# One read of each expert's weights: GpSimd rounds the high part by a copy and subtracts in place of a second, rounding transfer

## The chip, the cores and the metric

The kernel runs on one core of one Trainium2 chip. The metric is the device time of one execution in microseconds, as the median of several runs; lower is better. The engines are named as in the profile: PE is TensorE (PEld its weight loads), DVE is VectorE, ACT is ScalarE, POOL is GpSimd and SP is SyncE, which here only issues transfers.

## The reference, cut to what matters

A gated cross-attention block on x of 4 x 512 x 512 is followed by a mixture of experts. Every token goes to 4 of 16 experts; each expert is a gated feed-forward layer of width 352, and a shared one of width 704 runs for all tokens.

```python
x = x + tanh(g_xattn) * xattn(layernorm(x), ctx, ctx, wq, wk, wv, wo)
x = x + tanh(g_ffn) * moe(layernorm(x), Wg, W1, W2, W3, W1s, W2s, W3s)

# moe: 2048 tokens, 16 experts, top 4, D = 512, FF = 352
shared = silu(x @ W1s.T) * (x @ W3s.T) @ W2s.T
probs = softmax(x @ Wg.T);  topk_w, sel = top_k(probs, 4)
combine = zeros((T, E)).at[arange(T)[:, None], sel].add(topk_w)
h = silu(einsum('td,efd->etf', x, W1)) * einsum('td,efd->etf', x, W3)
routed = einsum('etf,edf->td', h * combine.T[:, :, None], W2)
return shared + routed
```

## The kernel before

The kernel keeps float32 accuracy with three products for each one: every operand is split into a high part, rounded to the type that PE multiplies (`fp32r`), and a low part, raw minus high; `tripled` (L80) issues high x high, low x high and high x low. For weights the high part comes from a transfer on POOL's queue that rounds on its way (`expert_hi`), the raw values from a second transfer of the same bytes (`expert_raw`), and POOL subtracts: `expert_lo = expert_raw - expert_hi`. `expert_raw` and `expert_lo` lie at one address, so the subtraction is in place.

There are four phases, each a block that all engines leave together. In attention (to about 458 us of the span) nothing here is touched. In the second phase, called routing (458 to 577 us; tiles and names with `b_`), PE runs the shared feed-forward for half of the tokens in two rounds n of six column groups j (the matmuls of one group write `b_ps_u`), then four outputs (`b_ps_y`). DVE multiplies gate and value of a group (L928, `b_h`), which also frees the PSUM buffer that PE's group after the next needs, and takes the low part of the group before (L917, `b_h_lo`, both inputs in SBUF). Between the groups DVE does the routing: at n = 0, j = 0 it ranks the experts of the last 512 tokens (L98 to L107, mostly with two inputs in SBUF) and makes `mask` (L1206), on which PE's counting matmuls ahead of group 3 wait (L1247); at j = 1 it makes the rest of the shared down weights' low part (L979); and so on, until lists of one-hot rows give every tile its tokens (`slot_tokens`). POOL in that time subtracts for the shared down weights (L979, 128x2560) and for the first expert (L964: 128x3840 and then 96x512), and issues loads.

In the third phase, experts (577 to 1061 us, `c_`), the tokens are sorted by expert into tiles of 128: 72 tiles here, four or five for each expert. For a tile t, PE transposes the gathered rows `xg` (L1447), multiplies with `expert_hi` and `expert_lo` (`c_ps_u`), does the down product of tile t - 2 and the transposes of tile t - 1. POOL runs one `step` for each tile, in order: wait until PE has transposed tile t, gather tile t + 4 into the buffer that this frees (L1338, an indirect transfer), and, where tile t is the first of its expert e, make the low part of expert e + 1 and issue the loads of expert e + 2. Three buffers of weights go round. All of POOL's transfers, gathers and weight loads, go through one queue. PE waits with `w_ready` for an expert's low part, and with `gathered` for a tile's rows.

The last phase (from 1077 us, `d_`) runs the shared feed-forward for the other half and adds up the experts' outputs.

Of the kernel before, what the change touches and what calls it, by code (L numbers as in the profile page):

```python
# [13 lines left out]
P = 128  # L14
B, S, D = 4, 512, 512
T = B * S
NT = T // P
IT = S // P
# [4 lines left out]
FT = FF - 2 * P  # L23
# [715 lines left out]
W13 = 2 * DC * FF  # L739
W2 = 2 * D  # L740
WE = W13 + W2 + D
# [207 lines left out]
def part(w, rows, base, start, n):  # L949

    return w[0:rows, base + start:base + start + n] if isinstance(base, int) else w[0:rows, bass.ds(base + start, n)]


def load_expert(eng, w, base, io, e, sem):

    eng.dma_start(part(w, P, base, 0, W13 + W2), io["we"][e]).then_inc(sem, 16)
    eng.dma_start(part(w, FT, base, W13 + W2, D), io["we_rest"][e]).then_inc(sem, 16)


def split_expert(eng, later, base, sem):  # L960

    for rows, start, n in ((P, 0, W13 + W2), (FT, W13 + W2, D)):
        hi, lo, raw = (part(w, rows, base, start, n) for w in (later.w_hi, later.w_lo, later.w_raw))
        last = eng.tensor_tensor(lo, raw, hi, ALU.subtract)  # L964
    last.then_inc(sem, 1)
# [16 lines left out]
def routing_phase(nc, io, mem, keep, later):  # L982


    with ExitStack() as c:
# [51 lines left out]
        def _(sp):  # L1037
# [17 lines left out]
            sp.wait_ge(keep["gathered"][0], 16)  # L1055
            load_expert(sp, later.w_raw, WE, io, 1, keep["second_raw_in"])


        @block.gpsimd
        def _(pool):  # L1060
# [15 lines left out]
            load_expert(pool, later.w_hi, 0, io, 0, hi_in["first"])  # L1076
# [3 lines left out]
            pool.wait_ge(hi_in["first"], 32)  # L1080
            pool.wait_ge(raw_in["first"], 32)
            split_expert(pool, later, 0, first_ready)

            pool.wait_ge(sh.t_free, 2 * IT)
            pool.wait_ge(hot_ready, 1)
            load_expert(pool, later.w_hi, WE, io, 1, keep["w_in"])
# [4 lines left out]
                ap=keep["index"][:, 0:1], axis=0)).then_inc(keep["gathered"][0], 16)  # L1091
        @block.scalar
        def _(act):
            sh.scalar(act)
# [174 lines left out]
def expert_phase(nc, io, mem, keep, later):  # L1269

    with ExitStack() as c:
# [62 lines left out]
        def _(pool):  # L1334
# [6 lines left out]
            def load(base, e):  # L1341

                load_expert(pool, later.w_hi, base, io, e, w_in)
                load_expert(pool, later.w_raw, base, io, e, w_in)

            def step(t, v):
# [9 lines left out]
                with pool.If(flag > 0):  # L1356
# [3 lines left out]
                    pool.wait_ge(w_in, e * 64 + 32)  # L1360
                    split_expert(pool, later, base, w_ready)
# [16 lines left out]
            pool.wait_ge(keep["second_raw_in"], 32)  # L1378
# [242 lines left out]
def program(nc, io, out):  # L1621
    mem = {k: nc.dram_tensor(k + "_dram", shape, F32, kind="Internal").ap() for k, shape in (
        ("x2", [T, D]), ("xn2", [T, D]), ("base", [T, D]), ("y", [(TILES_MAX + REST) * P, D]))}
    keep = persistent(nc)
    later = Later(nc, keep["end"])
    with ExitStack() as c:
# [6 lines left out]
        keep["w_in"], keep["second_raw_in"] = sem("w_in"), sem("second_raw_in")  # L1633
# [47 lines left out]
```

## Time and profile before

| what | us |
|---|---|
| median of 3 runs | 1194.11 |
| lowest and highest run | 1193.88, 1196.51 |
| span of the profiled execution | 1198.8 |
| PE busy | 1117.1 (93%) |
| DVE busy | 508.4 (42%) |
| POOL busy | 467.2 (39%) |
| ACT busy | 280.2 (23%) |
| read from HBM, written to it | 161.51 MB, 37.75 MB |

The profiled execution has no time of its own beside its span, 1198.8 us from its first instruction to its last; that is 4.7 us over the median and 2.3 us over the highest of the three runs. Times inside the profile are positions in that span. PE is busy for nearly all of it, so that what shortens the kernel is a stretch in which PE stands still or runs at a lower clock; the other engines matter by what they keep PE waiting for.

### The profile page before, as it was taken

The numbers are of one execution on the slowest core, as the hardware profiler recorded it, in microseconds if no ns is written. First come the engines' busy times: TensorE is split into PE (matmuls) and PEld (weight loads), VectorE is DVE, ScalarE is ACT, GpSimd is POOL, SyncE is SP. The second block draws the span as 40 slices with busy tenths as digits, with TensorE's granted clock in tenths as the row PEclk, the third lists the DMA queues.
The fourth block names the chain that finished last, engine by engine and source line by source line (L and its number), as shares of the span: only waits on it lengthen the run. The fifth ranks groups of instructions, "written<-read, shape, count | busy, mean of one in ns | idle before, by whom it ended". The sixth has DMA issues, their size and how long they took to land. (4 is left out here: it accounts for less than half of the span.)

```text
span 1198.8 us, 18625 instructions
## 1 busy us (share of the span) xinstructions
PE 1117.1 (93%) x5666; PEld 948.6 (79%) x5667; DVE 508.4 (42%) x994; ACT 280.2 (23%) x575; POOL 467.2 (39%) x464
## 2 busy tenths in 40 slices
PE   4999998999899968799889999999999999989998
PEld 3877876878687845677779999999999999977675
DVE  2243446336443454999212222222222222226847
ACT  1221121113112201211123333333333333321110
POOL 4610101200210223300564565565656665608752
PEclk9998998999899977999889999999999999999898
DMA  9411221221120517140856666665666656526775
GB/s 358 169 71 70 73 98 41 105 105 70 37 103 35 219 71 265 38 138 32 292 219 230 223 223 223 223 222 196 247 227 215 231 214 232 201 80 227 234 249 158
DMA packets 54208, 199.70 MB, mean 167 GB/s; under 512 B 7008, under 2 KB 7008, under 8 KB 45984
## 3 DMA queue, kind: packets, MB, share of 16 engines
q0 software_dynamic: 21184, 122.44, 29.3%
q1 hardware_dynamic: 22624, 57.98, 13.5%
q10 hardware_dynamic: 10368, 18.88, 4.2%
q8 instruction: 18, 0.29, 0.1%
q14 instruction: 14, 0.11, 0.0%
HBM read 161.51 MB, written 37.75 MB: 166 GB/s over the span
## 5 line engine op out<-in xcount | busy, mean ns | idle before, releaser
L86 PE MATMUL c_ps_u<-expert_hi,xT_hi 128*128 x576 | 192.6, 334 | 1.7 <-DVE xT_lo L1421 1.6
L86 PE MATMUL c_ps_u<-expert_hi,xT_lo 128*128 x576 | 185.9, 323 | 0.0
L86 PE MATMUL c_ps_u<-expert_lo,xT_hi 128*128 x576 | 185.6, 322 | 0.0
L964 POOL TENSOR_TENSOR expert_lo<-expert_raw,expert_hi (+2 forms) x32 | 156.0, 4896 | 19.8 <-issue 13.3
L86 PEld LDWEIGHTS c_ps_u<-expert_hi,xT_hi 128*128 128x128 f32 x576 | 108.8, 189 | 2.4 <-issue 2.3
L1435 DVE TENSOR_TENSOR hf<-c_ps_u,gate 128x352 f32<-128x352 f32 x72 | 37.7, 524 | 169.8 <-ACT gate L1410 169.8
L86 PEld LDWEIGHTS c_ps_u<-expert_lo,xT_hi 128*128 128x128 f32 x576 | 109.3, 190 | 0.0
L86 PEld LDWEIGHTS c_ps_u<-expert_hi,xT_lo 128*128 128x128 f32 x576 | 108.8, 189 | 0.0
L1425 DVE TENSOR_TENSOR hT_lo<-c_ps_h,hT_hi 128x256 fp32r<-128x256 f32 x72 | 30.5, 424 | 182.0 <-ACT hT_hi L1400 182.0
L73 POOL TENSOR_TENSOR idle<-idle 128x1 f32<-128x1 f32 x91 | 17.4, 191 | 225.9 <-PE c_ps_x L1447 141.9
L86 PE MATMUL c_ps_y<-expert_hi,hT_hi 128*128 (+1 forms) x216 | 92.5, 428 | 2.3 <-DVE hT_lo L1426 2.3
L86 PE MATMUL c_ps_y<-expert_lo,hT_hi 128*128 (+1 forms) x216 | 86.2, 399 | 0.0
L86 PE MATMUL c_ps_y<-expert_hi,hT_lo 128*128 (+1 forms) x216 | 86.2, 399 | 0.0
L1338 POOL DMA_INDIRECT xg<-xn_dram,column x72 | 71.4, 992 | 25.1 <-issue 19.8
L1572 POOL DMA_INDIRECT parts<-y_dram,token_slots x64 | 68.2, 1065 | 27.2 <-issue 19.2
L1410 ACT ACTIVATE gate<-c_ps_u 128x352 f32<-128x352 f32 x72 | 33.5, 465 | 180.9 <-PE c_ps_u L86 180.9
L1393 ACT ACTIVATE y<-c_ps_y 128x512 f32<-128x512 f32 x72 | 43.1, 599 | 114.6 <-PE c_ps_y L86 114.6
L407 DVE TENSOR_TENSOR q_lo<-ps_products,q_hi 128x512 fp32r<-128x512 f32 x32 | 22.1, 690 | 101.7 <-ACT q_hi L339 101.7
L339 ACT ACTIVATE q_hi<-ps_products 128x512 fp32r<-128x512 f32 x32 | 19.1, 598 | 154.4 <-PE ps_products L86 154.4
L1421 DVE TENSOR_TENSOR xT_lo<-c_ps_x,xT_hi 128x512 fp32r<-128x512 f32 x72 | 49.8, 691 | 12.6 <-ACT xT_hi L1387 9.3
L1599 DVE SCALAR_TENSOR_TENSOR total<-parts,combine_weights,total 128x512 f32<-128x512 f32 x64 | 48.0, 751 | 14.3 <-DMA total<-x_dram 8.1
L569 PE MATMUL ps_transposed<-ident,x_t 128*128 128x128 f32 x80 | 16.5, 357 | 40.0 <-DVE x_t L425 39.3
(268 smaller groups left out, 2480.1 us busy)
## 6 DMA issues: line engine op xcount, KB each, us to landing
expert_hi<-we POOLq DMA_DIRECT2D x16, 1920.0 KB, 7.9
expert_raw<-we POOLq DMA_DIRECT2D x14, 1920.0 KB, 13.0
y_dram<-y ACTq DMA_DIRECT2D x72, 256.0 KB, 2.1
ctxT_hi<-ctxT POOLq DMA_DIRECT2D x4, 1024.0 KB, 7.4
ctxT_raw<-ctxT SPq DMA_DIRECT2D x4, 1024.0 KB, 5.9
ctx_raw<-ctx SPq DMA_DIRECT2D x4, 1024.0 KB, 4.8
r_t<-x SPq DMA_DIRECT2D x4, 1024.0 KB, 5.4
ctx_hi<-ctx POOLq DMA_DIRECT2D x4, 1024.0 KB, 6.8
```

Of the source, the lines that this page charges most:

```text
L86: last = pe.matmul(out, a[i], b[j], start=(n == 0), stop=(n == 3 * len(pairs) - 1))
L339: act.activation(out, ps_m[:, (m.n - 1) % 2, :], ACT.Copy).then_inc(m_hi, 1)
L407: dve.tensor_tensor(lo, ps_m[:, (m.n - 1) % 2, :], hi, ALU.subtract).then_inc(m_free, 1)
L964: last = eng.tensor_tensor(lo, raw, hi, ALU.subtract)
L1338: pool.indirect_dma_start(xg[v][:], None, mem["xn2"], bass.IndirectOffsetOnAxis(ap=at, axis=0)).then_inc(gathered[v], 16)
L1393: act.activation(y[v][:], ps_y[:, v % 2, :], ACT.Copy).then_inc(y_taken, 1)
L1410: act.activation(gate[u][:], ps_u[:, u, 0, 0:FF], ACT.Silu).then_inc(gate_ready, 1)
L1421: dve.tensor_tensor(x[u][1][:], ps_x[:], x[u][0][:], ALU.subtract).then_inc(x_split, 1)
L1425: dve.tensor_tensor(h[u][1][:, 0:2, :], ps_h[:, 0:2, :], h[u][0][:, 0:2, :], ALU.subtract)
L1435: dve.tensor_tensor(hf[u][:], ps_u[:, u, 1, 0:FF], gate[u][:], ALU.mult).then_inc(h_ready, 1)
L1572: pool.indirect_dma_start(parts[v][:, q, :], None, y_d, bass.IndirectOffsetOnAxis(ap=keep["slots"][:, order[c], q:q + 1], axis=0)).then_in ...
L1599: ins = dve.scalar_tensor_tensor(out=total[k][:], in0=parts[c % 4][:, q, :], scalar=keep["weights"][:, order[c], q:q + 1], in1=total[k][:] ...
```

## The change

The rounding transfer of each expert's weights is gone: `expert_hi` is made by POOL, with `tensor_copy` from `expert_raw`, in the same two pieces as the subtraction. A wait on a new semaphore (`hi_made`) and a small instruction (`hold`) stand between the copies and the subtractions. The raw load of the second expert leaves SP, where it waited for the first gather, and is issued by POOL right behind that gather. POOL no longer waits for it ahead of the first tile, but in the first step.

```diff
-def split_expert(eng, later, base, sem):
-
+def split_expert(nc, keep, eng, later, base, expert, sem):
+
+    made = keep["hi_made"]
+    for rows, start, n in ((P, 0, W13 + W2), (FT, W13 + W2, D)):
+        hi, raw = (part(w, rows, base, start, n) for w in (later.w_hi, later.w_raw))
+        last = eng.tensor_copy(hi, raw)
+    last.then_inc(made, 1)
+    eng.wait_ge(made, expert + 1)
+    hold(nc, eng, keep, 6)
     for rows, start, n in ((P, 0, W13 + W2), (FT, W13 + W2, D)):
         hi, lo, raw = (part(w, rows, base, start, n) for w in (later.w_hi, later.w_lo, later.w_raw))
         last = eng.tensor_tensor(lo, raw, hi, ALU.subtract)
...
-            sp.wait_ge(keep["gathered"][0], 16)
-            load_expert(sp, later.w_raw, WE, io, 1, keep["second_raw_in"])
...
-            load_expert(pool, later.w_hi, 0, io, 0, hi_in["first"])
             pool.wait_ge(hi_in["down"], 32)
             pool.wait_ge(raw_in["down"], 32)
             split_down(pool, later.d_hi, later.d_lo, later.d_raw, True, down_ready)
-            pool.wait_ge(hi_in["first"], 32)
             pool.wait_ge(raw_in["first"], 32)
-            split_expert(pool, later, 0, first_ready)
-
-            pool.wait_ge(sh.t_free, 2 * IT)
-            pool.wait_ge(hot_ready, 1)
-            load_expert(pool, later.w_hi, WE, io, 1, keep["w_in"])
+            split_expert(nc, keep, pool, later, 0, 0, first_ready)
 
             pool.wait_ge(index_ready, 1)
             pool.wait_ge(sh.u_ready, 2 * SC)
             pool.indirect_dma_start(later.xg[0][:], None, mem["xn2"], bass.IndirectOffsetOnAxis(
                 ap=keep["index"][:, 0:1], axis=0)).then_inc(keep["gathered"][0], 16)
+            load_expert(pool, later.w_raw, WE, io, 1, keep["w_in"])
...
-                load_expert(pool, later.w_hi, base, io, e, w_in)
                 load_expert(pool, later.w_raw, base, io, e, w_in)
...
-                    pool.wait_ge(w_in, e * 64 + 32)
-                    split_expert(pool, later, base, w_ready)
+                    pool.wait_ge(w_in, e * 32 + 32)
+                    split_expert(nc, keep, pool, later, base, e + 1, w_ready)
...
-            pool.wait_ge(keep["second_raw_in"], 32)
             last = tiles(pool, step)
```

On POOL, at the place of the routing phase where the first expert is split, this stood before (`xg_69` is the first tile's gather, `slot_tokens` the list that it reads):

```order
L956 DMA expert_hi<-we 128x3840
L957 DMA expert_hi<-we_rest 96x512
L979 TENSOR_TENSOR shared_down_lo<-shared_down_raw,shared_down_hi 128x2560
L964 TENSOR_TENSOR expert_lo<-expert_raw,expert_hi 128x3840
L964 TENSOR_TENSOR expert_lo<-expert_raw,expert_hi 96x512
L956 DMA expert_hi<-we 128x3840
L957 DMA expert_hi<-we_rest 96x512
L1090 DMA xg_69<-xn_dram,slot_tokens 128x512
```

and this stands there now:

```order
L986 TENSOR_TENSOR shared_down_lo<-shared_down_raw,shared_down_hi 128x2560
L965 CAST expert_hi<-expert_raw 128x3840
L965 CAST expert_hi<-expert_raw 96x512
L73 TENSOR_TENSOR idle<-idle 128x1
L971 TENSOR_TENSOR expert_lo<-expert_raw,expert_hi 128x3840
L971 TENSOR_TENSOR expert_lo<-expert_raw,expert_hi 96x512
L1087 DMA xg_69<-xn_dram,slot_tokens 128x512
L956 DMA expert_raw<-we 128x3840
L957 DMA expert_raw<-we_rest 96x512
```

Two rounding loads are gone from here, two casts and a small instruction have come in ahead of the subtractions, and the second expert's raw load, from SP's queue, stands behind the gather.

On POOL, in the step of a tile that is the first of its expert, from the subtraction to the gather of the next step (the rows of registers and branches between are left out), this stood before:

```order
L964 TENSOR_TENSOR expert_lo<-expert_raw,expert_hi 128x3840
L964 ISA
L964 TENSOR_TENSOR expert_lo<-expert_raw,expert_hi 96x512
...
L956 DMA expert_hi<-we 128x3840
L957 ISA
L957 DMA expert_hi<-we_rest 96x512
L956 REGISTER_ALU
L956 DMA expert_raw<-we 128x3840
L957 REGISTER_ALU
L957 DMA expert_raw<-we_rest 96x512
...
L1338 DMA xg_70<-xn_dram,column_3353 128x512
```

and this stands there now:

```order
L965 COPY expert_hi<-expert_raw 128x3840
L965 ISA
L965 COPY expert_hi<-expert_raw 96x512
L967 REGISTER_ALU
L73 TENSOR_TENSOR idle<-idle 128x1
L971 TENSOR_TENSOR expert_lo<-expert_raw,expert_hi 128x3840
L971 TENSOR_TENSOR expert_lo<-expert_raw,expert_hi 96x512
...
L956 DMA expert_raw<-we 128x3840
L957 ISA
L957 DMA expert_raw<-we_rest 96x512
...
L1337 DMA xg_70<-xn_dram,column_3349 128x512
```

The next tile's gather now has two loads ahead of it in the queue instead of four, and two copies more ahead of it on the engine.

## Rows read from the trace of the kernel before

**Rows 1.** Stretch, its us, busy PE PEld DVE ACT POOL, clock, DMA share, GB/s.

```profile
630.00:1060.00 430.00, 430.00 (x2573) 400.36 (x2572) 117.35 (x256) 139.60 (x320) 249.71 (x294) 1.00 0.62 219
```

**Rows 2.** PE's waits: what ended them, us in total, times, longest.

```profile
PE c_ps_x L1447 <- DMA xg<-xn_dram,column: 4.5, 1, 4.5
```

**Rows 3.** PE's timeline, transposes of tiles 3 to 6 of the experts.

```profile
597.66 0.60 PE L1447 MATMUL c_ps_x<-ident,xg 128*128 128x128 f32 x4
604.36 0.60 PE L1447 MATMUL c_ps_x<-ident,xg 128*128 128x128 f32 x4
615.78 1.11 PE L1447 MATMUL c_ps_x<-ident,xg 128*128 128x128 f32 x4 [4.50 <-DMA xg<-xn_dram,column]
624.75 0.60 PE L1447 MATMUL c_ps_x<-ident,xg 128*128 128x128 f32 x4
```

**Rows 4.** The same view as rows 1, behind PE's wait in the experts.

```profile
615.78:622.00 6.22, 6.22 (x23) 5.11 (x24) 0.69 (x1) 1.26 (x3) 4.22 (x4) 0.63 0.24 77
```

**Rows 5.** POOL's timeline at the start of the experts.

```profile
577.28 0.98 POOL L1338 DMA_INDIRECT xg<-xn_dram,slot_tokens  x1 [0.17 <-issue]
...
585.88 0.19 POOL L1349 COPY column<-slot_tokens 128x1 int32<-128x1 int32 x1 [5.12 <-DMA expert_raw<-we_rest]
...
589.75 9.76 POOL L964 TENSOR_TENSOR expert_lo<-expert_raw,expert_hi  x2 [1.88 <-issue]
...
601.24 0.54 POOL L957 DMA_DIRECT2D expert_raw<-we_rest  x1
...
602.81 1.01 POOL L1338 DMA_INDIRECT xg<-xn_dram,column  x1 [0.50 <-issue]
```

**Rows 6.** Transfers issued from 599 to 603 us: KB, us from issue to landing.

```profile
expert_hi<-we_rest POOLq DMA_DIRECT2D x1, 192.0 KB, 9.0
expert_raw<-we_rest POOLq DMA_DIRECT2D x1, 192.0 KB, 13.8
```

**Rows 7.** Landing of the gather issued at 602.81 us.

```profile
DMA to landing us min/median/max: 12.9/12.9/12.9
```

**Rows 8.** SP's queue at the end of routing: start, us.

```profile
575.25 0.43 SPq L956 DMA_DIRECT2D expert_raw<-we  x1
```

**Rows 9.** POOL's casts in the profile before: us in total, mean ns.

```profile
L1074 POOL CAST lane<-lane_i 128x128 f32<-128x128 int32 x1 | 0.3, 298 | 0.0
L1075 POOL CAST token<-token_i 128x16 f32<-128x16 int32 x1 | 0.2, 202 | 0.0
```

**Rows 10.** POOL's timeline in routing, 470 to 495 us.

```profile
470.46 5.71 POOL L979 TENSOR_TENSOR shared_down_lo<-shared_down_raw,shared_down_hi 128x2560 fp32r<-128x2560 f32 x1 [8.05 <-DMA shared_down_hi<-d_rest]
482.68 10.07 POOL L964 TENSOR_TENSOR expert_lo<-expert_raw,expert_hi 128x3840 fp32r<-128x3840 f32 x2 [6.52 <-DMA expert_raw<-we_rest]
```

**Rows 11.** DVE's timeline in the same stretch.

```profile
472.11 5.14 DVE L98 TENSOR_TENSOR b_rank_level<-probs 128x1024 f16<-128x1024 f32 x1
...
478.54 1.23 DVE L102 TENSOR_TENSOR b_rank_level<-probs 128x1024 f16<-128x1024 f32 x1
...
481.78 0.23 DVE L107 TENSOR_TENSOR ranks<-b_rank_larger,b_rank_equal 128x64 f32<-128x64 f32 x1
...
482.25 0.68 DVE L928 TENSOR_TENSOR b_h<-b_ps_u,b_silu 128x512 f32<-128x512 f32 x1
482.85 8.78 DVE L917 TENSOR_TENSOR b_h_lo<-b_h,b_h_hi 128x512 fp32r<-128x512 f32 x1
...
493.33 0.69 DVE L928 TENSOR_TENSOR b_h<-b_ps_u,b_silu 128x512 f32<-128x512 f32 x1
```

**Rows 12.** PE's timeline there: the wait of group 4.

```profile
494.08 0.80 PE L86 MATMUL b_ps_u<-b_xT_hi,shared_up_hi 128*128 128x512 f32 x1 [5.32 <-DVE b_h L928]
```

**Rows 13.** The same view as rows 1, routing's start and behind PE's wait.

```profile
458.00:482.00 24.00, 21.65 (x88) 17.15 (x86) 13.09 (x11) 5.64 (x9) 9.94 (x14) 0.82 1.03 366
...
494.08:497.50 3.42, 3.42 (x8) 2.75 (x9) 3.25 (x8) 0.61 (x1) 0.00 (x0) 0.50 0.00 0
```

**Rows 14.** First expert's last raw piece, issued from SP at 460.8 us.

```profile
expert_raw<-we_rest SPq DMA_DIRECT2D x1, 192.0 KB, 21.8
```

More of the change, by code:

```diff
@@ L1632, in program @@
         keep["y_out"], keep["base_out"] = [sem(f"y_out{v}") for v in range(QUAD)], [sem(f"base_out{u}") for u in range(2)]
-        keep["w_in"], keep["second_raw_in"] = sem("w_in"), sem("second_raw_in")
+        keep["w_in"], keep["hi_made"] = sem("w_in"), sem("hi_made")
         keep["last_down_in"], keep["last_xs_in"] = sem("last_down_in"), [sem(f"last_xs{i}_in") for i in range(IT)]
```

## The prediction

> **What bounds the kernel now.** I read first the busy times by stage. From 630 to 1060 us PE is busy for 430.00 of 430 us at the full granted clock [rows 1]. Nothing that POOL or the transfers do can shorten that part; it can only break it. So I looked for the places where PE stands still and where POOL's work or the weight loads have a hand in it. The list of PE's waits and its timeline give two.
>
> The first is in the experts. PE waits 4.5 us for a gather of rows, once, and nowhere else there [rows 2]. The timeline shows what that costs in all: the transposes of tile 3 and tile 4 stand 604.36 - 597.66 = 6.70 us apart, which is the length of a tile, while from tile 4 to tile 6 it takes 624.75 - 604.36 = 20.39 us instead of 13.40 [rows 3]. The tile costs 7.0 us too much: 4.5 of waiting, and about 2.5 more at a lower clock (0.63 of full on average behind the wait [rows 4]). The gather is late because of POOL. POOL waited 5.12 us for the second expert's raw load, subtracted for 9.76 us, issued four loads and only then, at 602.81, this gather [rows 5]. It landed 12.9 us later [rows 7], at 615.7, which is 0.7 us behind the last piece of those loads (601.24 + 13.8 = 615.0 [rows 5, 6]).
>
> The second is in routing. PE waits 5.32 us for DVE's `b_h` of group 2 [rows 12] and then runs 3.4 us at 0.50 of the clock [rows 13], so at 1.2 instead of 2.4 GHz, which loses 1.7 us. DVE is late because its instructions with two inputs in SBUF stood still while POOL subtracted: L98 took 5.14 us beside POOL's 5.71 us subtraction and ended 1.1 us behind it, though its twin L102 takes 1.23; L917 took 8.78 us beside POOL's next one [rows 10, 11]. DVE came through its ranking undisturbed only because POOL's second subtraction began at 482.68, right behind `b_h` of group 1 at 482.25.
>
> **The change in the experts.** SP no longer issues two transfers at the end of routing; they began at 575.25, each of some 0.43 us [rows 8], and with the gap between them the end of the phase comes 0.9 us earlier. POOL then does not stand for 5.12 us, so its first `column` copy, at 585.88 before, comes at 585.88 - 5.12 - 0.9 = 579.9, and its first work on weights 3.87 us later (589.75 - 585.88 [rows 5]), at 583.7. The data are there by then: the raw load is issued before the phase ends, by 575 at the latest, and an unburdened load's last piece lands 9.0 us after issue [rows 6].
>
> The price of the copies is what the trace does not show at this size. The lower bound is from POOL's casts: (298 - 202) ns for (128 - 16) elements is 0.86 ns per element [rows 9], which makes 3.5 us for 128x3840 and 0.6 us for 96x512, 4.1 us together. The upper bound is that a copy costs as much as the subtraction of the same size, 9.76 us for both [rows 5]; that instruction reads twice as much, so I take 4.1. The wait on `hi_made` and `hold` add 0.4 us, an estimate from the 0.50 us that POOL idles between such a small instruction and the gather at 602.81 [rows 5].
>
> So the copies end at 587.8, the subtractions run from 588.2 to 598.0. Before, the last raw piece was issued 1.73 us and the gather 3.30 us after the subtractions' end; with two issues of about 0.55 us fewer this is 0.6 and 2.2 us. The raw load's last piece lands at 598.6 + 9.0 = 607.6, the gather, again 0.7 us behind it, at 608.3. PE wants it at 604.36 + 6.70 - 0.9 = 610.2. The margin is 1.9 us: the stall goes, -7.0 us, and the earlier end of routing gives -0.9.
>
> For the other experts the chain from one load to the next is copies 4.1, 0.4, subtractions 9.76, issue 0.6, landing 9.0: 23.9 us, against 4 x 6.70 = 26.8 us for the shortest experts. It stays hidden under PE, and so do the gathers, which have half as many bytes ahead of them. Were that cover gone (the upper bound makes it 29.6), each such expert would bring POOL 2.8 us later.
>
> **The change in routing.** One load of 1920 + 192 KB fewer competes. The stretch from 458 to 482 moved 366 GB/s [rows 13], so 2.16 MB are worth 5.9 us, and the first expert's last raw piece, at 460.8 + 21.8 = 482.6 before [rows 14], lands at about 476.7. POOL's down subtraction ends at 476.17 [rows 10]. Hence POOL starts on the expert at about 477.3, behind DVE's waiting L98, and not at 482.68. That is worse for DVE, whose whole ranking now runs beside it. One after the other, by the rows and with the port changing hands at each instruction: copy to 480.8; L102 (ready at 478.54) to 482.0; second copy to 482.6; L103 to 483.3; POOL's large subtraction, 8.3 us (482.68 to 482.85 + 8.78 - 0.68), from 483.4 to 491.7; only then L107, ready long ago, then `mask`, and `b_h` of group 1 at 493.0 instead of 482.9 [rows 11]. PE's group 3 needs both and starts 10.1 us late. Group 4's wait of 5.32 us is no longer there, since `b_h` of group 2 follows within 3 us. Net +4.8, and 0.4 for a somewhat longer stretch at the lower clock behind a wait twice as long: +5.2 us.
>
> Whether a copy, with its one input, holds DVE off too, no row shows; only subtractions do. The Trainium skill (GPSIMD Engine Reference, section 8, Key points) says that GpSimd shares its SBUF interfaces with VectorE, in contention with VectorE's instructions that have two inputs in SBUF, and makes no exception for GpSimd's one-input ones. By it the copies block and the sum stays as above; it is a rule against this change. With the subtractions alone blocking, the term is +2.5 (first rival).
>
> **Sum.** -7.0 - 0.9 + 5.2 = -2.7 us. The profiled span of 1198.8 becomes 1196.1. The span lies 4.7 us over the median of the runs, and the same difference put on 1194.1 gives 1191.4. Its own range, for copies of 4 to 6 us and a raw load that lands within 2 us of my time, is 1188.5 to 1194.5. A difference under 0.2% (2.4 us) can't be told from none.
>
> **Rivals.**
> - Copies do not hold DVE. They run at 476.7 to 480.8, the large subtraction from 481.2 to 489.5 still catches L107 (ready at 481.78), `b_h` of group 1 ends at 490.7, 7.8 us late, less 5.3: +2.5. Time 1188.7. For it: no row of a one-input POOL instruction that stops DVE. Against: all long POOL instructions in the trace did.
> - The raw load lands late, after 482.3. Then DVE's ranking passes, `b_h` of group 2 slips in between the copies and the large subtraction, and PE waits about 3.3 us at group 5 in place of 5.3 at group 4: -2 and -1 for the clock, with the experts' -7.9 that is -10.9 in all, 1183.2. Against it is the sum of bytes.
> - Slower: the copies are dear. Each us over 4.1 costs one in routing, and each beyond the margin of 1.9 another in the experts. The gain is used up at copies of 6.4 us; over 0.2% slower begins at 7.6. At the upper bound routing costs +10.9 and the stall is 3.8 + 2.5 of the old 7.0: 1194.1 + 10.9 - 0.7 - 0.9 = 1203.4, more if four-tile experts in a row fall behind.
> - The gather stays late although the copies are cheap, because a raw load with stores of zeros and gathers beside it lands later than 9.0 + 1.9 us. Then up to the whole 7.0 stays: 1194 to 1198.4.
>
> **Chances.** Forecast 0.45, copies that don't hold DVE 0.19, late raw load 0.07, dear copies 0.17, late gather 0.12. Below 1191.7 lie a little over half of the forecast's case (0.25) and the first two rivals: 0.51 faster. Within 0.2% lie the rest of it and some of the last two: 0.31. Slower 0.18. The range 1186 to 1199 leaves out the late load and the upper end of dear copies.
>
> **What would show it.** In the changed kernel's timeline: the large copy 3.5 us long; no wait of PE on `xg` near 611; POOL's expert work in routing starting at 477 and not 483; L102 stretched to about 3.5 us; L107 ending near 492; one PE wait of about 11 us ahead of the counting matmul and none at group 4; 430 us of unbroken PE afterwards. The prediction is wrong if the copy is 6 us or more, if the first raw load lands after 482, or if POOL's subtraction leaves L107 alone.

## The result, and the profile after

The change made the kernel slower: a median of 1199.77 us (15 runs) against 1196.09 us of the kernel before, run beside it (15 runs; the three runs that stand in the table above had 1194.11). The ratio is 1.0033, with a 95% interval of 1.002 to 1.0046, so 3.9 us. The profiled span went from 1198.8 to 1200.3 us; that pair alone is a poor measure, since single executions of one kernel differ by some us with the granted clock.

The page of the kernel after: busy time, share, instructions, and the bytes.

```profile
PE 1114.9 (93%) x5666; PEld 946.8 (79%) x5667; DVE 509.8 (42%) x994; ACT 279.9 (23%) x575; POOL 516.0 (43%) x482
HBM read 126.91 MB, written 37.75 MB: 137 GB/s over the span
L965 POOL CAST expert_hi<-expert_raw (+2 forms) x32 | 64.2, 2034 | 17.3 <-issue 15.4
```

34.6 MB fewer are read, and POOL is busy for 48.8 us more, less than the 64.2 us of the copies, since it issues 15 pairs of loads fewer, of some 1.15 us each. PE's waits, from 452 to 1090 us (what ended them, us in total, times, longest):

```profile
PE b_ps_y L1246 <- DVE mask L1205: 10.5, 1, 10.5
PE c_ps_x L1444 <- PEq L992: 6.7, 1, 6.7
PE c_ps_x L1444 <- DMA xg<-xn_dram,column: 0.6, 1, 0.6
```

The third line answers to [rows 2]: the 4.5 us for the gather at tile 5 are gone; the 0.6 us are another tile's, near the end. The first was 0.8 us before and stands in place of group 4's 5.32 us [rows 12]. The second was 2.6 us before and is the one that my prediction had not asked about: `PEq` is PE's own sequencer, which stands at the end of the routing block until all engines have left it.

I cut the time of PE into stages by marks that both kernels have: the first `b_ps_u` matmul behind the first transposes, the last `b_ps_y` matmul of routing, the first transposes of the experts, those of tile 1 and of the last tile (tiles are counted from 0). "Gap" is from the last routing matmul to the first transposes of the experts.

| us | before | after | difference |
|---|---|---|---|
| routing | 109.94 | 115.02 | +5.1 |
| gap | 3.01 | 7.11 | +4.1 |
| tile 0 | 8.23 | 8.70 | +0.5 |
| tile 1 to last tile | 474.96 | 469.79 | -5.2 |
| the four together | 596.14 | 600.62 | +4.5 |

What lies ahead of these stages is untouched by the change. In the two profiles it was 1.6 us shorter in after, and behind the experts 1.4 us shorter; both vary as much between executions of other kernels below without following any edit.

POOL and then DVE in the kernel after, in routing; the rows answer to [rows 10, 11]. Start and duration.

```profile
467.76 5.71 POOL L986 TENSOR_TENSOR shared_down_lo<-shared_down_raw,shared_down_hi 128x2560 fp32r<-128x2560 f32 x1 [7.96 <-DMA shared_down_hi<-d_rest]
475.38 4.94 POOL L965 CAST expert_hi<-expert_raw 128x3840 fp32r<-128x3840 f32 x2 [1.92 <-DMA expert_raw<-we_rest]
480.40 0.52 POOL L73 TENSOR_TENSOR idle<-idle 128x1 f32<-128x1 f32 x1
480.88 9.47 POOL L971 TENSOR_TENSOR expert_lo<-expert_raw,expert_hi 128x3840 fp32r<-128x3840 f32 x2
```

```profile
475.83 4.02 DVE L102 TENSOR_TENSOR b_rank_level<-probs 128x1024 f16<-128x1024 f32 x1
479.89 0.98 DVE L103 TENSOR_TENSOR b_rank_level<-b_rank_level,b_lower_index 128x1024 f16<-128x1024 f16 x1
480.90 1.22 DVE L106 TENSOR_REDUCE b_rank_equal<-b_rank_level 128x64 f32<-128x1024 f16 x1
482.16 7.07 DVE L107 TENSOR_TENSOR ranks<-b_rank_larger,b_rank_equal 128x64 f32<-128x64 f32 x1
489.26 1.25 DVE L1205 TENSOR_SCALAR mask<-ranks 128x256 f16<-128x256 f32 x1
```

L102, 1.23 us before, takes 4.02 beside a copy with one input (it starts 0.45 us behind the copy, whose large piece lasts 3.39 us); L107, 0.23 us of work, waits out the large subtraction. The end of the block, POOL first, then the landings of what it issued there (KB, us from issue to landing), then PE:

```profile
573.72 1.07 POOL L1087 DMA_INDIRECT xg<-xn_dram,slot_tokens  x1 [83.36 <-DVE slot_tokens L1228]
574.80 0.62 POOL L956 DMA_DIRECT2D expert_raw<-we  x1
575.39 0.57 POOL L957 DMA_DIRECT2D expert_raw<-we_rest  x1
584.18 0.52 POOL L1334 MEMSET zeros<- 128x512 f32 x1 [8.22 <-POOLq L992]
```

```profile
expert_raw<-we POOLq DMA_DIRECT2D x1, 1920.0 KB, 7.9
expert_raw<-we_rest POOLq DMA_DIRECT2D x1, 192.0 KB, 8.3
```

```profile
577.11 0.39 PE L86 MATMUL b_ps_y<-shared_down_hi,b_h_lo 64*128 64x512 f32 x1
584.22 1.09 PE L1444 MATMUL c_ps_x<-ident,xg 128*128 128x128 f32 x4 [6.73 <-PEq L992]
...
612.42 0.60 PE L1444 MATMUL c_ps_x<-ident,xg 128*128 128x128 f32 x4
619.35 0.60 PE L1444 MATMUL c_ps_x<-ident,xg 128*128 128x128 f32 x4
```

The load's last piece lands at 575.39 + 8.3 = 583.7, and POOL and PE start again at 584.2. The same place in the kernel before, SP's issue, its landing, and POOL:

```profile
575.72 0.45 SPq L957 DMA_DIRECT2D expert_raw<-we_rest  x1
expert_raw<-we_rest SPq DMA_DIRECT2D x1, 192.0 KB, 10.1
576.58 0.53 POOL L1335 MEMSET zeros<- 128x512 f32 x1 [5.26 <-POOLq L985]
```

Before, SP issued that piece at 575.72, it landed 10.1 us later, at 585.8, and all engines had started again at 576.6, without waiting for it. So my first reading was: the end of the block waits for the landing of transfers that POOL has issued, and not for those of SP. The last two lines of PE above answer to [rows 3]: tile 4 and tile 5 are 6.93 us apart.

### The profile page after: what moved, and what is told of

The parts are those of the page before. It is cut to its first block and busy times, and to the rows that moved or that the text cites. A ratio compares the mean times of both kernels' runs of the same rounds, so it can differ in the third digit from the quotient of the medians.

```text
span 1200.3 us, 18597 instructions
## 1 busy us (share of the span) xinstructions
PE 1114.9 (93%) x5666; PEld 946.8 (79%) x5667; DVE 509.8 (42%) x994; ACT 279.9 (23%) x575; POOL 516.0 (43%) x482
## 3 DMA queue, kind: packets, MB, share of 16 engines
q1 hardware_dynamic: 22368, 55.81, 12.9%
## 5 line engine op out<-in xcount | busy, mean ns | idle before, releaser
L73 POOL TENSOR_TENSOR idle<-idle 128x1 f32<-128x1 f32 x107 | 21.0, 196 | 173.6 <-PE c_ps_x L1444 88.4
L965 POOL CAST expert_hi<-expert_raw (+2 forms) x32 | 64.2, 2034 | 17.3 <-issue 15.4
L1596 DVE SCALAR_TENSOR_TENSOR total<-parts,combine_weights,total 128x512 f32<-128x512 f32 x64 | 53.8, 840 | 15.0 <-DMA total<-x_dram 8.7
L292 POOL TENSOR_TENSOR ln_rstd<-ln_var,minus_half 128x4 f32<-128x4 f32 x8 | 8.3, 1034 | 109.6 <-DVE ln_var L420 109.6
```

What stands on the lines that cost most here:

```text
L965: last = eng.tensor_copy(hi, raw)
L1596: ins = dve.scalar_tensor_tensor(out=total[k][:], in0=parts[c % 4][:, q, :], scalar=keep["weights"][:, order[c], q:q + 1], in1=total[k][:] ...
```

## The experiments

All stand beside the kernel before, in three groups of four, each on its own chip. The difference in us is the ratio put on 1196; "four stages" is the sum of the stages above, less that of before, from each kernel's one profile.

| kernel | median | ratio [95%] | us | routing | gap | tile 0 | tiles 1 to last | four stages |
|---|---|---|---|---|---|---|---|---|
| before | 1196.0 to 1196.6 | | | 109.94 | 3.01 | 8.23 | 474.96 | |
| after | 1199.77 | 1.0033 [1.002, 1.0046] | +3.9 | 115.02 | 7.11 | 8.70 | 469.79 | +4.5 |
| e1_sp_load | 1199.94 | 1.0032 [1.0016, 1.0048] | +3.8 | 115.12 | 6.05 | 9.14 | 469.22 | +3.4 |
| e2_before_pool_load | 1195.48 | 1.0001 [0.9986, 1.0016] | +0.1 | 109.31 | 8.36 | 9.14 | 469.46 | +0.1 |
| e3_pieces | 1195.94 | 1.0002 [0.9984, 1.002] | +0.2 | 109.68 | 7.46 | 9.40 | 469.83 | +0.2 |
| e4_after_mask | 1199.05 | 1.0023 [1.0007, 1.0038] | +2.8 | 112.44 | 7.45 | 8.12 | 470.90 | +2.8 |
| e7_sp_as_before | 1197.12 | 1.0008 [0.9992, 1.0025] | +1.0 | 114.93 | 3.01 | 8.74 | 469.68 | +0.2 |
| e8_pool_next_phase | 1202.16 | 1.0052 [1.0032, 1.0072] | +6.2 | 115.04 | 2.04 | 11.38 | 473.20 | +5.5 |
| e9_pieces_sp | 1188.53 | 0.995 [0.9934, 0.9966] | -6.0 | 109.58 | 3.01 | 8.38 | 470.18 | -5.0 |
| e10_only_experts | 1188.94 | 0.9941 [0.9921, 0.9962] | -7.1 | 109.47 | 3.02 | 8.46 | 469.17 | -6.0 |
| e11_copies_pieces | 1188.24 | 0.9931 [0.9911, 0.995] | -8.3 | 110.02 | 3.01 | 8.40 | 470.52 | -4.2 |
| e12_subs_pieces | 1190.12 | 0.9941 [0.992, 0.9962] | -7.1 | 108.56 | 3.00 | 8.60 | 471.44 | -4.5 |
| e13_behind_gathers | 1198.43 | 1.001 [0.9992, 1.0028] | +1.2 | 109.48 | 2.04 | 8.60 | 478.51 | +2.5 |
| e14_before_sub_pieces | 1190.18 | 0.9939 [0.9918, 0.9961] | -7.3 | 108.99 | 3.00 | 8.51 | 469.71 | -5.9 |

The stages of single profiles explain the measured differences to 1.4 us but for e11 and e12, which measured 4.1 and 2.5 us faster than their stages say; their intervals are +-2.3 and +-2.5 us wide. Differences of 1 to 2 us between the kernels from e9 to e14 aren't resolved.

### The second raw load from SP, early (e1_sp_load)

```diff
+                if k == 2 * IT - 1:
+                    sp.wait_ge(index_ready, 1)
+                    load_expert(sp, later.w_raw, WE, io, 1, keep["second_raw_in"])
                 sp.wait_ge(sh.y_free, k + 1)
...
                 ap=keep["index"][:, 0:1], axis=0)).then_inc(keep["gathered"][0], 16)
-            load_expert(pool, later.w_raw, WE, io, 1, keep["w_in"])
```

> The changed kernel, with the second expert's raw load issued by SP as soon as the slot list is ready, ahead of its last store, instead of by POOL behind the first gather. Theory (the end of the routing phase waits until the transfers that POOL issued have landed): the gap on PE between the last matmul of routing and the first transposes of the experts falls from 7.1 us to 2 to 3 us, the wait of 10.5 us ahead of the counting matmul stays, and the kernel comes out 4 to 6 us faster than the changed one, so 0 to 2 us under the kernel before. Rival (the gap comes from something else at that place, such as the load's traffic or a late last store): the gap stays near 7 us and the time near +3.9 us.

The gap was 6.05 us and the time that of the changed kernel, as the rival had it. SP's last piece, then POOL, and the landings:

```profile
575.83 0.47 SPq L957 DMA_DIRECT2D expert_raw<-we_rest  x1
```

```profile
575.71 1.07 POOL L1090 DMA_INDIRECT xg<-xn_dram,slot_tokens  x1 [83.43 <-DVE slot_tokens L1230]
585.11 0.53 POOL L1336 MEMSET zeros<- 128x512 f32 x1 [8.33 <-POOLq L992]
```

```profile
expert_raw<-we_rest SPq DMA_DIRECT2D x1, 192.0 KB, 10.5
xg<-xn_dram,slot_tokens POOLq DMA_INDIRECT x1, 9.0
```

POOL now has one transfer outstanding, the first gather. With SP's load just ahead of it, it takes 9.0 us to land and not 3.4; it lands at 584.7, SP's load at 586.3, and the engines start at 585.1, behind the first and ahead of the second. So the load was moved off POOL's queue and the gap stayed, as a gather's late landing. This run doesn't tell the queues apart by its time, only by this order of landings.

### The load alone, put into the kernel before (e2_before_pool_load)

```diff
-            sp.wait_ge(keep["gathered"][0], 16)
-            load_expert(sp, later.w_raw, WE, io, 1, keep["second_raw_in"])
...
                 ap=keep["index"][:, 0:1], axis=0)).then_inc(keep["gathered"][0], 16)
+            load_expert(pool, later.w_raw, WE, io, 1, keep["second_raw_in"])
```

> The kernel before, with only this: the second expert's raw load is issued by POOL behind the first gather, and not by SP. Theory (phase end waits for POOL's transfers to land): PE's gap between routing and experts grows from 3.0 us to about 7 us. Since the load has then landed when the experts start, POOL no longer stands 5.1 us for it, the gather of tile 5 comes about 5 us earlier against PE, and the stall of 7.0 us at tile 5 should shrink to under 1 us; in all -2 to -3 us against the kernel before. Rival (the gap has another cause): the gap stays at 3 us and the time falls by 7 us.

POOL issues the last piece and starts again in the next block:

```profile
569.96 0.59 POOL L957 DMA_DIRECT2D expert_raw<-we_rest  x1
580.02 0.53 POOL L1332 MEMSET zeros<- 128x512 f32 x1 [9.47 <-POOLq L985]
```

The piece landed after 9.4 us, at 579.4, 0.7 us ahead of that start. The gap became 8.36 us, 5.3 us more than before, with no copy in the kernel. The edit also takes 5.5 us of the stall at tile 5 away (tiles 469.46), but all engines now spend about as much in the gap. Both cancel, and the ratio is 1.0001; I had 2 to 3 us less than before.

### First expert's work in pieces (e3_pieces)

```diff
+    pieces = [(P, at, 480) for at in range(0, W13 + W2, 480)] + [(FT, W13 + W2, D)]
-    for rows, start, n in ((P, 0, W13 + W2), (FT, W13 + W2, D)):
+    for rows, start, n in pieces:
         ...
         last = eng.tensor_copy(hi, raw)
...
-    for rows, start, n in ((P, 0, W13 + W2), (FT, W13 + W2, D)):
+    for rows, start, n in pieces:
         ...
         last = eng.tensor_tensor(lo, raw, hi, ALU.subtract)
```

> The changed kernel, with the first expert's copies and subtractions cut into pieces of 480 columns (8 of each in place of one), nothing else. Theory (a POOL instruction holds off a DVE instruction with two inputs in SBUF until it ends, and the two take turns): no such DVE instruction waits more than about 1.3 us, PE's wait of 10.5 us ahead of the counting matmul falls under 2 us and the wait at group 4 of the kernel before does not come back; 10 to 12 us faster than the changed kernel, 6 to 8 us under the kernel before. Rival (DVE is held while POOL has work queued, whatever its pieces, or is slowed in proportion): the wait of PE stays at 8 us or more and the time within 2 us of the changed kernel's.

The wait for the mask falls from 10.5 to 0.4 us. Routing is 5.3 us shorter, not 10: a wait of 3.8 us for `b_h_lo`, later in the phase, comes in. It stands in e9_pieces_sp too, whose rows (PE, then DVE) are:

```profile
499.41 0.50 PE L86 MATMUL b_ps_y<-shared_down_hi,b_h_hi 128*128 128x512 f32 x1 [3.23 <-DVE b_h_lo L917]
```

```profile
487.73 0.53 DVE L1125 COPY r_s<-r_totals 128x256 f32<-128x256 f32 x1
488.30 1.07 DVE L1127 COPY r_s<-r_s 128x16 f32<-128x16 f32 x1
489.29 0.40 DVE L1128 TENSOR_TENSOR r_s<-r_s 128x240 f32<-128x240 f32 x1
489.71 1.08 DVE L1127 COPY r_s<-r_s 128x32 f32<-128x32 f32 x1
...
498.68 0.68 DVE L917 TENSOR_TENSOR b_h_lo<-b_h,b_h_hi 128x512 fp32r<-128x512 f32 x1
```

Behind the mask DVE has some 10 us of small steps for the slots, from 487.7 to 498.1, before it comes to `b_h` and `b_h_lo`. It is busy all that time, but three of the steps (two are shown), copies of 0.2 us in the kernel after, take 1.1 us and a fourth, of 0.35 us, takes 1.5 beside the pieces of the subtraction, 3.8 us too much in all. The hold is spread over these steps and not gone: from `b_h` of group 4 to the end of the next `b_h_lo` DVE takes 13.6 us, against 9.5 in after, and PE waits 3.2 us and then 0.6 more.

### The copies held back until the mask is made (e4_after_mask)

```diff
+            pool.wait_ge(mask_ready, 1)
             split_expert(nc, keep, pool, later, 0, 0, first_ready)
```

> The changed kernel, with POOL waiting for DVE's mask before it starts the first expert's copies. Theory (it was the start of POOL's work, 5.8 us earlier than before, that caught DVE's ranking): the wait ahead of the counting matmul falls from 10.5 us to about 1; DVE's low parts are then held by the copies and by the large subtraction, and PE waits some 3 us at group 4 or 5; 6 to 9 us faster than the changed kernel, 2 to 5 us under the kernel before. Rival (the copies' added 4 us of POOL work are the cause, wherever they lie): PE's waits in routing stay at 9 us or more in sum.

The wait for the mask is gone; waits of 3.1 us for `b_h` and 2.2 for `b_h_lo` are there, since the large instructions now hold DVE at those. Routing 112.44 us: half of the 5.1 us is back, and the time is 1.1 us under the changed kernel's, not 6 to 9. When the large instructions run decides which of DVE's is late, and none of these places is free.

### The second raw load from SP, as before (e7_sp_as_before)

```diff
+            sp.wait_ge(keep["gathered"][0], 16)
+            load_expert(sp, later.w_raw, WE, io, 1, keep["second_raw_in"])
...
                 ap=keep["index"][:, 0:1], axis=0)).then_inc(keep["gathered"][0], 16)
-            load_expert(pool, later.w_raw, WE, io, 1, keep["w_in"])
```

> The changed kernel, but the second expert's raw values are loaded by SyncE, at the place of the kernel before: behind the last store, once the first gather has landed. Theory (the end of the routing phase waits for the landing of what GpSimd has issued, and not for what SyncE has issued): the gap from the last routing matmul to the first expert matmul falls from 7.1 to 3.0 us, and the kernel takes 4 us less than the changed one, about 1195.7 us, a ratio of 1.000 to the kernel before. Rival (the end waits for the load's landing whoever issues it, or something else of the change lengthens the gap): it stays at 6 to 8 us and the time at about 1199.8. In both the stall at tile 5 stays away (experts 469 to 471 us from the second tile to the last).

The gap is 3.01 us again, to the hundredth, with all else as in the changed kernel, and the tiles stay at 469.68. SP, then POOL:

```profile
576.35 0.45 SPq L957 DMA_DIRECT2D expert_raw<-we_rest  x1
```

```profile
577.21 0.53 POOL L1336 MEMSET zeros<- 128x512 f32 x1 [5.27 <-POOLq L992]
...
586.24 3.94 POOL L965 CAST expert_hi<-expert_raw  x2 [2.86 <-DMA expert_raw<-we_rest]
```

The block ends 0.4 us behind SP's last issue, and 9 us before the load is used. The time, +1.0 us with an interval of -1.0 to +3.0, agrees with the four stages (+0.2) and with 4 us less than the changed kernel, though the interval doesn't fix it.

### The same load as POOL's first transfer in the next block (e8_pool_next_phase), and behind the gathers there (e13_behind_gathers)

```diff
+            load_expert(pool, later.w_raw, WE, io, 1, w_in)     (e8)
             for v in range(1, QUAD):
                 gather(v, keep["index"][:, v:v + 1])
+            load_expert(pool, later.w_raw, WE, io, 1, w_in)     (e13)
```

> The changed kernel, but GpSimd issues the second expert's raw load as the first of its transfers in the expert phase, ahead of the gathers for tiles 1 to 3. Theory: neither SyncE's two issues nor a landing stand at the end of the routing phase, the gap is 2.1 us (3.0 less the 0.9 us of SyncE's two issues), and the kernel takes 5 us less than the changed one, 1194.8, unless the gathers of tiles 1 to 3 now land behind the load and TensorE waits for them (up to 5 us at tile 1). Rival (the gap has another cause): 6 us or more.

> The first expert's copies and subtractions in pieces, and the second raw load issued by GpSimd in the expert phase, behind the gathers of tiles 1 to 3. Theory: the gap is 2.1 us as when the load was the first transfer of that phase, and the gathers of tiles 1 to 3 are no longer behind the load, so the first tiles take 8.4 and 6.1 us again; the second expert's split ends some 5 us later than with SyncE's load, at about 602, in time for its tile. 1187.6, a ratio of 0.994. Rival (the gathers of the later tiles, issued behind the later split and beside the next load, land late): a TensorE wait of 4 us or more at tile 5, time 1192 or later.

e13 has the pieces of e3 as well. In both the gap is 2.04 us: with neither SP's two issues nor a landing there, the 0.9 us of my prediction are to be had, and were measured as 0.97. In neither kernel is it worth it. In e8 PE waits for tile 1's gather, which stands behind the load:

```profile
590.63 0.66 PE L1444 MATMUL c_ps_x<-ident,xg 128*128 128x128 f32 x4 [3.63 <-DMA xg<-xn_dram,slot_tokens]
```

With it, a further wait of 2.2 us in tile 1 and the lower clock there (0.63 of full, against 1.00 in after) tiles 0 and 1 take 2.7 and 3.2 us more than in after, and the kernel is the slowest of all. In e13 tile 0 takes its 8.60 us, but the old stall is back, bigger. POOL, then PE:

```profile
592.53 3.95 POOL L965 CAST expert_hi<-expert_raw  x2 [10.59 <-DMA expert_raw<-we_rest]
...
606.52 0.59 POOL L956 DMA_DIRECT2D expert_raw<-we  x1
607.12 0.55 POOL L957 DMA_DIRECT2D expert_raw<-we_rest  x1
...
608.70 1.03 POOL L1351 DMA_INDIRECT xg<-xn_dram,column  x1 [0.49 <-issue]
```

```profile
616.70 1.12 PE L1459 MATMUL c_ps_x<-ident,xg 128*128 128x128 f32 x4 [7.08 <-DMA xg<-xn_dram,column]
```

The load, behind three gathers and beside the stores of zeros, took 13.1 us to land instead of 8.3, POOL waited 10.59 us for it, and the gather was issued at 608.70, 0.9 us ahead of the moment at which PE wanted its rows (616.70 - 7.08 = 609.6). My theory there (split ended by 602) was wrong by 4.4 us, and the rival was right. The margin of this gather is a few us whichever way the load goes.

### Both mends (e9_pieces_sp)

e3's pieces and e7's load.

> The changed kernel with both mends: the first expert's copies and subtractions in pieces of 480 columns, and the second raw load by SyncE as in the kernel before. Theory (the two costs are apart from each other and add up): the routing phase 109.7 us, the gap 3.0, experts 469.8, so 1195.9 less 4.4 = 1191.5 us, a ratio of 0.996 to the kernel before. Rival (what is taken from the gap comes back elsewhere, as a longer first stretch at the lower clock or a late gather): 1194 to 1196, ratio 0.999 to 1.000.

Ratio 0.995 (0.9934 to 0.9966), 6.0 us under the kernel before and 10 us under the changed one. Routing 109.58, gap 3.01: the two costs are apart from each other, as the theory had it, and the gain of the experts stays.

### The change in the expert phase alone (e10_only_experts)

Routing as in the kernel before, with the first expert's rounding load, and SP's load as before; the rest as changed:

```diff
+            load_expert(pool, later.w_hi, 0, io, 0, hi_in["first"])
...
+            pool.wait_ge(hi_in["first"], 32)
...
-            split_expert(nc, keep, pool, later, 0, 0, first_ready)
+            for rows, start, n in ((P, 0, W13 + W2), (FT, W13 + W2, D)):
+                hi, lo, raw = (part(w, rows, 0, start, n) for w in (later.w_hi, later.w_lo, later.w_raw))
+                last = pool.tensor_tensor(lo, raw, hi, ALU.subtract)
+            last.then_inc(first_ready, 1)
```

> The kernel before in its routing phase (first expert's rounded part loaded, not copied; second raw load by SyncE) with the change in the expert phase alone: raw read once, copy, subtraction in place. Theory: routing 109.9 us, gap 3.0 less what the one load fewer frees (0 to 0.3), experts 469.8 in place of 475.0: 5.2 us less than before, 1190.9 us, ratio 0.9957. Rival (the copies hold VectorE in the expert phase as in the routing phase, or the lower clock takes the gain back): experts 472 us or more, 1193.5 or later.

Ratio 0.9941 (0.9921 to 0.9962), 7.1 us under the kernel before (I had 5.2). Tile 0 and the rest together take 477.63 us in place of 483.19: 5.6 us less. From 630 to 1060 us:

```profile
630.00:1060.00 430.00, 429.55 (x2565) 399.21 (x2564) 117.35 (x256) 139.43 (x320) 289.74 (x306) 1.00 0.44 154
```

Against [rows 1] the bytes are down from 219 to 154 GB/s and POOL is busy for 40 us more, and PE loses 0.45 us: the copies cost PE next to nothing in this stretch, the bytes saved bring it nothing, since it was busy for all of it before, and the whole gain is the one stall.

What takes the stall away can be read here too. The gather of tile 5:

```profile
601.88 1.01 POOL L1344 DMA_INDIRECT xg<-xn_dram,column  x1 [0.49 <-issue]
```

It is issued 0.9 us earlier than before (602.81 [rows 5], with both blocks starting at the same time to 0.1 us), and lands 7.6 us later, at 609.5, where before it took 12.9 us [rows 7], to 615.7. So 5.3 of the 6.2 us come from the shorter queue ahead of the gather, one load instead of two. With one load ahead it took 7.3 us in e9 and 8.0 in e13, with two 12.9 in e2 as well, where the stall went because POOL issued the gather 3.1 us earlier in the block. In the kernel at hand POOL waits for the raw load in the first step and not ahead of the first tile, 2.98 us in place of 5.12, and with the copies it issues the next load 23.15 us after the block's start, against 22.99 before. The load's move to POOL was not needed for any of this.

### Which large instruction holds DVE (e11_copies_pieces, e12_subs_pieces)

Both are e9 with one of its two loops whole again: in e11 the subtractions are whole, in e12 the copies.

```diff
-    for rows, start, n in pieces:
+    for rows, start, n in ((P, 0, W13 + W2), (FT, W13 + W2, D)):
```

> As the kernel with both mends, but only the first expert's copies are in pieces of 480 columns; its two subtractions are whole. Theory (the large copies hold VectorE's comparison until they end, and so push the last step of the ranking behind the start of the large subtraction): with the copies in pieces the ranking is through before the subtraction starts, TensorE's wait for the mask is under 1 us, and the large subtraction holds VectorE later, at a b_h_lo of the shared expert, as in the kernel before: a wait of some 5 us there, routing 110 to 113 us, 1190 to 1193. Rival (the subtraction alone delays the ranking, the copies' form does not matter): a wait for the mask of 8 us or more, routing 115, 1195.

> As the kernel with both mends, but only the first expert's subtractions are in pieces of 480 columns; its two copies are whole. Theory: the copy of 3.4 us still holds the second comparison of the ranking until it ends, but the last step of the ranking then waits for one piece and not for the whole subtraction: a wait for the mask of 2 to 4 us, routing 110.5 to 113 us, 1190 to 1192.5. Rival (copies do not hold VectorE): no wait for the mask, routing 109.6, 1188.5.

DVE in e11, then in e12:

```profile
475.19 1.43 DVE L102 TENSOR_TENSOR b_rank_level<-probs 128x1024 f16<-128x1024 f32 x1
...
478.91 0.30 DVE L107 TENSOR_TENSOR ranks<-b_rank_larger,b_rank_equal 128x64 f32<-128x64 f32 x1
...
482.98 8.39 DVE L917 TENSOR_TENSOR b_h_lo<-b_h,b_h_hi 128x512 fp32r<-128x512 f32 x1
```

```profile
475.78 3.04 DVE L102 TENSOR_TENSOR b_rank_level<-probs 128x1024 f16<-128x1024 f32 x1
...
481.13 1.15 DVE L107 TENSOR_TENSOR ranks<-b_rank_larger,b_rank_equal 128x64 f32<-128x64 f32 x1
482.32 1.19 DVE L1222 TENSOR_SCALAR mask<-ranks 128x256 f16<-128x256 f32 x1
```

With the copies in pieces L102 takes 1.43 us, the ranking is through at 479.2, before the large subtraction starts, and no wait for the mask is left; the subtraction then holds `b_h_lo` for 8.39 us, nearly as in [rows 11]. With whole copies L102 takes 3.04 us and PE waits 4.4 us for the mask (I had 2 to 4). So copies do hold DVE. Yet both kernels' routing is at 110.02 and 108.56 us, level with e9's 109.58. In e11 PE waits 4.3 us behind the subtraction, against 4.0 in e9 in all; e12's 4.4 us of waiting cost nothing at all against e9. With PE that late, DVE's small steps come behind POOL's last piece (491.8) and take their 0.2 us each, and PE no longer waits for `b_h_lo`.

### Subtraction in pieces, no copy (e14_before_sub_pieces)

e10 with its large subtraction in eight pieces.

> The change in the expert phase alone (routing phase and loads as in the kernel before), and the first expert's subtraction in pieces of 480 columns. Theory (the wait of 3.2 us for b_h_lo that is left in the routing phase comes from the large subtraction): the wait goes, routing 106.5 us in place of 109.5, 1186, a ratio of 0.991. Rival (VectorE's own work in the routing phase is what TensorE waits for there, as in the kernel with pieces, where a wait of 3.8 us stands with no large instruction beside it): routing 109.5, 1189.

A wait of 2.5 us for `b_h_lo` is left of 3.2, and routing is 108.99 us. My 3 us did not come: with no long instruction beside it, PE still waits there. But three of DVE's small copies take 1.08, 1.08 and 1.17 us beside the pieces, nearly as in e9, 2.8 us too much together, about the length of the wait.

The rival (DVE's own work alone) falls by the other kernels. Where these small steps run undisturbed and start on time (after, e1, e7, e8, e12), DVE takes 9.5 us from `b_h` of group 4 to the end of the next `b_h_lo`, and PE never waits for it. In e3, e9, e13 and e14 it takes 12.9 to 13.6 us, and PE, which wants the result 10.4 to 10.5 us after that `b_h`, waits 2.5 to 3.2. In e2, e10 and e11 it takes 9.8 us but starts late, behind a `b_h_lo` that POOL's large subtraction held for over 8 us, and PE waits 3.1 to 3.2 (e4 is of this kind, with 1.6, as PE had waited for `b_h` already). So DVE's own chain has 0.9 us to spare, and it is POOL's work that makes PE wait, by holding one long instruction or by stretching the short ones.

## Why the prediction was wrong, and where right

I had forecast 1191.4 us, 2.7 under before, and it is 3.7 over. The kernel before measured 2.0 us higher here than in the three runs that I set out from; the other 6.4 us are of the sum, and in the four stages, where -2.7 stands against +4.5, they are 7.2.

- **The step that failed** is the end of the routing phase: "SP no longer issues two transfers at the end of routing [...] and with the gap between them the end of the phase comes 0.9 us earlier", with the raw load "issued before the phase ends" at no cost. The gap went from 3.01 to 7.11 us: +4.1 for -0.9, 5.0 us of the 7.2. SP's two issues are indeed worth 0.97 us (e8, e13). But the block's end waits for what POOL has outstanding, and the load that the change puts there lands 8.3 us after issue. The prediction's own numbers (issued by 575 at the latest, 9.0 us to land) had the load under way well past the end of the phase, and priced that at nothing. The kernel before with the load alone (e2) gained 5.3 us of gap; the change with the load back on SP (e7) had 3.01. All seven kernels with SP's load in its old place have 3.00 to 3.02, whatever POOL's splits look like. I had the row that shows the rule in reach (SP's load is still under way when the engines start again at 576.6) and took it for a rule of all transfers.
- **The wait that it replaced.** POOL's 5.12 us wait for the raw load [rows 5] cost PE nothing by itself, only through the late gather of tile 5; in the changed kernel the same landing is waited for by every engine. And in the changed kernel it bought nothing: with the load back on SP (e7, e10) POOL waits 2.9 and 3.0 us for it, issues the gather 25.2 and 25.4 us after the block's start, against 25.9 in after and 26.2 before, and the stall is gone as well. I had 24.5, since I took the full 5.12 us off; in after POOL's copies start 9.75 us behind the block's start, not 8.0.
- **The routing term** was right: +5.2 forecast, +5.1 measured. The first raw piece was there at 475.3 (I had 476.7; this profile runs 1.6 us ahead of the other, so that is 476.9), the second comparison was held by the copy, L107 by the subtraction, and the one wait ahead of the counting matmul is 10.5 us (about 11). e11 and e12 show that copies hold DVE, against the first rival. The mends show that no such wait is simply saved: five forms of POOL's work (e9 to e12, e14) lie between 108.6 and 110.0 us, with PE's waits at the mask, at `b_h` or at `b_h_lo`. DVE's own chain behind group 4 would fit (9.5 of 10.4 us), so what is left there is POOL's work, 10 us of it or more, which holds DVE somewhere in every form. How short routing would be with POOL idle stays open, as no kernel does that; e14 less its one such wait is 106.5 us, an estimate.
- **The copy's price** was right: 3.41 us for 128x3840 and 3.94 for both pieces alone (3.5 and 4.1 forecast), so the dear copies' rival falls. Where the trace has 4.94 us for both, in routing, they take turns with DVE.
- **The experts' term** had the right mechanism and was mis-sized: -7.0 forecast. The stall at tile 5 gave 6.8 of it back; tile 0 takes 0.5 us more, and tiles 68 and 69, near the end, take 1.6 us more, 0.6 of it a wait for a gather. That makes -4.7, and 2.3 us of the 7.2. I had neither. The 0.5 us of tile 0 follow no edit: it takes 8.74 us in e7, with the short gap, and 8.12 in e4, with the long one. Tiles 68 and 69 take 1.1 to 1.8 us more in all the kernels that copy in this phase and nothing more in e2, which does not, so it comes with the change in this phase; what makes up the part that is no wait for a gather stays open. In the kernels with the change and the short gap the term is -3.2 (e12) to -5.6 (e10). The last rival, that the gather stays late, did not happen in after; e13 shows what it costs when it does, a wait of 7.1 us.

For the slower outcome I had the dear copies as the mechanism. It was slower for another cause, which no case of mine held.

**What to keep of the change.** The single read in the expert phase with SP's load in its place is 6 to 8 us faster than the kernel before, in five forms (e9 to e12, e14) that these measurements don't rank. Of the splits in routing either form will do: the rounding load as before, or copy and subtraction with one of the two in pieces.

## What to carry to other kernels

A transfer that is issued ahead of the end of a block costs the time to its landing if it is on the queue that the block's end waits for; look in the trace for transfers still under way when the engines start again, and from which queue they are. A wait that an edit takes from one engine is worth nothing until it is known who waits for the same landing instead. And when one engine serves another through many small steps, taking out its longest wait exposes the next one: price an edit by the length of the whole chain, not by the wait that the list shows.

## What was unexpected of the hardware

- The end of a block waited for POOL's transfers and not for SP's. Before: SP's last piece, issued at 575.72, landed at 585.8; all engines went on at 576.6. After: POOL's, issued at 575.39, landed at 583.7; they went on at 584.2. e1: POOL's gather landed at 584.7, SP's load at 586.3; they went on at 585.1. Whether it is POOL's instruction at the block's end or the queue's kind that makes the wait no run here tells apart.
- A gather of 128 rows lands 3.4 us after issue by itself, 9.0 us beside 2 MB that another queue had just issued (e1, 575.45 to 576.30, the gather at 575.71): two queues don't keep them apart. Behind loads on its own queue, a gather took 7.6 us with one load just ahead of it (e10) and 12.9 with two [rows 7].
- One-input instructions take part as well, on both sides. A one-input copy on POOL stretched a comparison on DVE from 1.2 to 4.0 us, and DVE's one-input `mask` took 1.25 us in after and 0.57 in e9, against 0.29 in e14, where it runs with POOL idle. Not all of DVE's do: L106, a one-input reduction, took 1.22 us beside POOL's large subtraction in after, as it did before with POOL idle. The Trainium skill (SBUF - State Buffer, Who interferes with whom) says that the two engines share one pair of ports, which whoever starts first holds for its whole instruction; the holds of e11 and e12, which end with the single copy or the single piece, agree with that.
- Cutting POOL's work into pieces costs little: in e9 eight copies and a small one took 6.84 us against 4.94 in after, nine subtractions 12.18 against 9.47, DVE's turns included.
